# Tridiagonalisation of a 1024 x 1024 matrix in one kernel: other steps for the last two tiles, another order of waits

## What is computed

```python
deg = sum(A, 0) + sum(A, 1) - diagonal(A)
L_norm = dinv[:, None] * (diag(deg) - A) * dinv[None, :]
_, U = eigh(L_norm)
h = relu(einsum('mn,bnd->bmd', U.T, x) @ W1 + b1)
out = einsum('nm,bmd->bnd', U, h @ W2 + b2)
```

## Time and profile before

| | |
|---|---|
| median of 3 runs | 9817.23 us (9799.33 to 9818.49) |
| profiled execution | 9792.26 us, of which the span is 9790.5 us |
| VectorE busy | 7098.8 us (73% of the span) |
| TensorE busy | 5600.1 us (57%) |
| ScalarE, GpSimd busy | 1776.4 us (18%), 1185.3 us (12%) |
| tridiagonalisation | about 900 to 6010 us from the span's start |
| its stages of T = 3, 2, 1 | 4441 to 4977, 4986 to 5505, 5512 to 6005 us |
| granted clock, whole span | 0.746 of 2.4 GHz |

### The profile page before, as it was taken

One profiled execution on the slowest core, in us unless ns is written; L12 is line 12 of the kernel. 1 busy time (PEld: TensorE's weight loads), 2 busy tenths in 40 slices (PEclk: granted clock), 3 DMA queues, 4 the chain that ended last, 5 costly groups with the idle time before them and its releaser, 6 DMA issues. The chain is left out here.

```text
span 9790.5 us, 326141 instructions
## 1 busy us (share of the span) xinstructions
PE 5600.1 (57%) x136408; PEld 3949.5 (40%) x136408; DVE 7098.8 (73%) x33446; ACT 1776.4 (18%) x4691; POOL 1185.3 (12%) x5177
## 2 busy tenths in 40 slices
PE   5675888777878777778777764121111110047866
PEld 2354555555566666566656653010000000033355
DVE  3555666767777777777777778989898989954154
ACT  1432111111111111111111111121111110011055
POOL 0000111111222222222222221000000000000000
PEclk8898999999999999786655555555555555579988
DMA  1000000000000000000000000000000000000000
GB/s 35 1 0 18 4 4 4 4 4 4 4 4 4 4 4 4 4 4 4 4 4 4 3 3 2 0 0 0 0 0 0 0 0 0 0 0 1 17 0 17
DMA packets 24594, 41.92 MB, mean 4 GB/s; under 512 B 2464, under 2 KB 20128, under 8 KB 23200
## 3 DMA queue, kind: packets, MB, share of 16 engines
q1 hardware_dynamic: 23200, 21.70, 0.7%
HBM read 17.50 MB, written 4.19 MB: 2 GB/s over the span
## 5 line engine op out<-in xcount | busy, mean ns | idle before, releaser
L289 PE MATMUL tri_y<-L 128*32 128x256 f32 (+7 forms) x36792 | 1941.3, 343 | 18.7 <-issue 17.7
L289 PEld LDWEIGHTS tri_y<-L 128*32 128x32 f32 x36792 | 1187.9, 122 | 241.9 <-issue 66.3
L1342 PE MATMUL ev_agree<-ev_prod,ev_fold 128*128 128x448 bf16 x520 | 241.3, 567 | 1683.5 <-DVE ev_prod L1465 1666.9
L1342 PEld LDWEIGHTS ev_agree<-ev_prod,ev_fold 128*128 128x128 bf16 x520 | 34.8, 111 | 1887.8 <-DVE ev_prod L1465 1867.4
L314 PE MATMUL tri_ring<-ident 128*128 128x128 bf16 x7414 | 750.3, 268 | 2.1 <-issue 1.9
L1458 DVE SCALAR_TENSOR_TENSOR ev_seq<-ev_seq,ev_ne2G,ev_u 128x112 f32<-128x112 f32 x2048 | 686.1, 335 | 73.3
L1454 DVE SCALAR_TENSOR_TENSOR ev_u<-ev_x,ev_dG,ev_seq 128x112 f32<-128x112 f32 x2048 | 683.9, 334 | 64.0
L272 PE MATMUL tri_k<-tri_kp,tri_half 128*32 128x1 f32 x8176 | 264.8, 189 | 759.7 <-DVE tri_x L476 755.8
L364 ACT ACTIVATE tri_mu<-tri_ring,tri_tiny 128x1 f32<-128x1 f32 x1022 | 267.4, 262 | 2172.6 <-PE tri_ring L272 2172.6
L314 PEld LDWEIGHTS tri_ring<-ident 128*128 128x128 bf16 x7414 | 582.1, 121 | 171.0 <-issue 155.6
L366 ACT ACTIVATE tri_sM<-tri_half_M,tri_s 128x8 f32<-128x8 f32 (+7 forms) x1022 | 304.2, 298 | 1823.4 <-DVE tri_s L468 1823.4
(11 more groups left out here) (615 smaller groups left out, 12957.9 us busy)
## 6 DMA issues: line engine op xcount, KB each, us to landing
adj<-in_adj_dram SPq DMA_DIRECT2D x12, 1024.0 KB, 8.1
x<-in_x_dram SPq DMA_DIRECT2D x8, 512.0 KB, 7.2
out_dram<-x SPq DMA_DIRECT2D x8, 512.0 KB, 6.6
gcn_w<-in_L_gnn_W_dram SPq DMA_DIRECT2D x2, 128.0 KB, 2.1
spec_w<-in_L_gnn_W_dram SPq DMA_DIRECT2D x2, 64.0 KB, 1.9
dot_wt<-in_L_gnn_W_dram SPq DMA_DIRECT2D x1, 64.0 KB, 1.8
dot_rows<-in_L_gnn_b_lin_dram SPq DMA_DIRECT2D x1, 64.0 KB, 2.7
dot_rows<-in_L_gnn_b_dram SPq DMA_DIRECT2D x1, 64.0 KB, 3.7
```

Source lines behind the costliest of these rows:

```text
L289: last = nc.tensor.matmul(y[32 * g:32 * g + 32, 0:T * 32], A[:, b + t, XC:XC + 1].broadcast_to([P, 32]), cols, start=(t == 0), stop=(t == ...
L1342: last = nc.tensor.matmul(agree, fold16[:, :], prod[:, z, h * (GRP // 2):(h + 1) * (GRP // 2), :].rearrange("p s w -> p (s w)"), start=Fal ...
```

## The change

For T of 1 and 2 (`few`) the step is written anew. The norm follows x directly, ahead of w. TensorE makes the sum twice, into two banks (`sigma` for ScalarE, `sigma_v` for VectorE), and then the products, ahead of rows and coefs; there is no filler. The flag is made from the second sum while the root is under way. `sgn2` and `aa` take the place of S2. `rows` and `coefs` stay, BnS goes to GpSimd, whose fB, nB and Bc go away for one product Cf = flag times Cw; fB is now on VectorE, followed by z, q1 = z - Bn and q. Kappa comes from TensorE as a sum of products of gx and t itself, over T matmul groups, and c from gx and zh, which ScalarE makes from t; the half and the flag in them are in `s4[:, s, 1:2]` and `vmc`. One instruction more per panel (kS) scales the kappas. L476 and L479 have no counterpart.

For T = 3 the norm follows x directly too, and one product stands ahead of the sum, as for T of 4 and more already. For all T of 3 and more: the flag is written behind S2; kappa's wait is written ahead of vm's, c's ahead of v's, and on ScalarE inv's ahead of xm's. The numbers of fillers for T = 3 to 6 are unchanged.

The core of the diff:

```diff
+FILL = {6: 8, 5: 10, 4: 10, 3: 10}
...
+        few = lambda T: T <= 2
+        norm_first = lambda T: T <= 3
+        idle = lambda T: FILL.get(T, 0)
...
+                        if few(T):
+                            pool.wait_ge(fl_ready, r + 1)
+                            nc.gpsimd.tensor_scalar(Cf[:, b:NT], Cw[:, b:NT, s], fl[:, s:s + 1], None, ALU.mult).then_inc(Cf_ready, 1)
+                            if s:
+                                pool.wait_ge(sum_ready, r + 1 if s0 else r)
+                                nc.gpsimd.tensor_tensor(col, Cw[:, b:NT, s], rowsum[:, b:NT], ALU.add).then_inc(Bn_ready, 1)
+                        else:
+                            pool.wait_ge(Bn_ready, r + 1)
+                            nc.gpsimd.tensor_scalar(fB[:, b:NT], col, fl[:, s:s + 1], None, ALU.mult).then_inc(pool_step, 1)
+                            pool.wait_ge(pool_step, 3 * r + 1)
+                            nc.gpsimd.tensor_tensor(nB[:, b:NT], fB[:, b:NT], col, ALU.subtract).then_inc(pool_step, 1)
...
-                        early = 0 if T < 4 else 1
-                        for t in range(early):
-                            product(t)
+                        first = T if T <= 2 else 1
+                        if not few(T):
+                            for t in range(first):
+                                product(t)
                         pe.wait_ge(norm_part, r + 1)
                         four(sigma, ones[:, 0:32], part[:, :]).then_inc(norm_ready, 1)
+                        if few(T):
+                            four(sigma_v, ones[:, 0:32], part[:, :]).then_inc(norm_again, 1)
+                            for t in range(first):
+                                product(t)
...
-                        for t in range(early, T):
+                        for t in range(first, T):
                             product(t)
-                        if T <= 6:
-                            for _ in range(8 if T == 6 else 10):
-                                nc.tensor.matmul(ring[3][:, 0:P], S["ident16"][:, :], S["ident16"][:, :], start=True, stop=True)
-                        pe.wait_ge(kappa_part, r + 1)
-                        four(kappa(s), half[:, 0:32], kp[:, :]).then_inc(kappa_ready, 1)
-                        four(c_sum, half[:, 0:32], kp[:, :], stop=False)
+                        for _ in range(idle(T)):
+                            nc.tensor.matmul(ring[3][:, 0:P], S["ident16"][:, :], S["ident16"][:, :], start=True, stop=True)
+                        if few(T):
+                            pe.wait_ge(t_ready, r + 1)
+                            pe.wait_ge(gx_ready, r + 1)
+                            tm = t1 if s else tr[:, 0:NT * 32].rearrange("p (t m) -> p t m", m=32)[:, :, 0]
+                            t0 = b if s else 0
+                            for t in range(T):
+                                last = four(kappa(s), gx[:, b + t:b + t + 1].broadcast_to([P, 32]), tm[:, t0 + t:t0 + t + 1], start=(t == 0), stop=(t == T - 1))
+                            last.then_inc(kappa_ready, 1)
+                            pe.wait_ge(zh_ready, r + 1)
+                            for t in range(T):
+                                four(c_sum, gx[:, b + t:b + t + 1].broadcast_to([P, 32]), zh[:, b + t:b + t + 1], start=(t == 0), stop=False)
+                        else:
+                            pe.wait_ge(kappa_part, r + 1)
+                            four(kappa(s), half[:, 0:32], kp[:, :]).then_inc(kappa_ready, 1)
+                            four(c_sum, half[:, 0:32], kp[:, :], stop=False)
...
-                        act.wait_ge(s4_ready, r + 1)
-                        nc.scalar.activation(sM[:, b:NT], half_M[:, s, 0:T], ACT.Copy, scale=s4[:, s:s + 1]).then_inc(sM_ready, 1)
+                        if not few(T):
+                            act.wait_ge(s4_ready, r + 1)
+                            nc.scalar.activation(sM[:, b:NT], half_M[:, s, 0:T], ACT.Copy, scale=s4[:, s, 0:1]).then_inc(sM_ready, 1)
+                        act.wait_ge(inv_ready, r + 1)
                         act.wait_ge(xm_ready, r + 1)
-                        act.wait_ge(inv_ready, r + 1)
                         nc.scalar.activation(vm[:, b:NT], xm[:, b:NT], ACT.Copy, scale=inv[:, 1:2]).then_inc(vm_ready, 1)
+                        if few(T):
+                            act.wait_ge(s4_ready, r + 1)
+                            act.wait_ge(vm_ready, r + 1)
+                            nc.scalar.activation(vmc[:, b:NT], vm[:, b:NT], ACT.Copy, scale=s4[:, s, 1:2]).then_inc(vmc_ready, 1)
+                            tm = t1[:, b:NT] if s else tr[:, 0:T * 32].rearrange("p (t m) -> p t m", m=32)[:, :, 0]
+                            act.wait_ge(t_ready, r + 1)
+                            nc.scalar.activation(zh[:, b:NT], tm, ACT.Copy, scale=s4[:, s, 1:2]).then_inc(zh_ready, 1)
...
+                    def norm(r):
+                        if r:
+                            dve.wait_ge(x_ready, r)
+                        X = xcol(b)
+                        V_.tensor_tensor_reduce(out=x2[:, act_t], in0=X, in1=X, scale=1.0, scalar=0.0, op0=ALU.mult, op1=ALU.add,
+                                                accum_out=part[:, 0:1]).then_inc(norm_part, 1)
+                    if norm_first(T):
+                        norm(0)
...
+                        if few(T):
+                            pre = r + 1 if s0 else r
+                            dve.wait_ge(pivot_ready, r + 1)
+                            k_sg = mark(V_.tensor_scalar(sg[:, :], pivot(s)[:, 1:2], 0.0, -0.5, ALU.is_ge, ALU.add))
+                            dve.wait_ge(norm_again, r + 1)
+                            V_.tensor_scalar(f1, pivot(s)[:, 1:2], pivot(s)[:, 1:2], sigma_v, ALU.mult, ALU.is_lt).then_inc(fl_ready, 1)
+                            dve.wait_ge(root_ready, r + 1)
+                            mark(V_.reciprocal(rt[:, :], mu[:, :]))
+                            after(k_sg)
+                            mark(V_.tensor_scalar(sgn2[:, :], sigma_v, sg[:, :], None, ALU.mult))
+                            kk = mark(V_.scalar_tensor_tensor(out=aa[:, :], in0=mu[:, :].broadcast_to([P, 2]), scalar=sg[:, :], in1=pivot(s), op0=ALU.mult, op1=ALU.add))
+                            if s:
+                                dve.wait_ge(rows_ready, pre)
+                                k_b = mark(V_.tensor_tensor(c3(prodb), v_w(b)[:, :, :, 0:s], spread(rows(s)), ALU.mult))
+                            after(kk)
+                            kk = mark(V_.scalar_tensor_tensor(out=pair[:, s, :], in0=rt[:, :].broadcast_to([P, 2]), scalar=sgn2[:, :], in1=aa[:, :], op0=ALU.mult, op1=ALU.add))
+                            if s:
+                                dve.wait_ge(coefs_ready, pre)
+                                k_c = mark(V_.tensor_tensor(c3(prodc), v_w(b)[:, :, :, 0:s], spread(coefs(s)), ALU.mult))
+                                after(k_b)
+                                V_.tensor_reduce(rowsum[:, act_t], c3(prodb), mybir.AxisListType.XY, ALU.add).then_inc(sum_ready, 1)
+                            after(kk)
+                            V_.reciprocal(inv[:, :], pair[:, s, :]).then_inc(inv_ready, 1)
+                            if s:
+                                after(k_c)
+                                k_c = mark(V_.tensor_reduce(corr[:, act_t], c3(prodc), mybir.AxisListType.XY, ALU.add))
                             dve.wait_ge(mv_ready, r + 1)
+                            ins = V_.transpose(tr[:, 0:T * 32], y[:, 0:T * 32])
+                            if s:
+                                k_t = mark(ins)
+                            else:
+                                ins.then_inc(t_ready, 1)
+                            dve.wait_ge(inv_ready, r + 1)
+                            V_.scalar_tensor_tensor(out=gx[:, act_t], in0=X, scalar=inv[:, 0:1], in1=H_, op0=ALU.mult, op1=ALU.add).then_inc(gx_ready, 1)
+                            dve.wait_ge(fl_ready, r + 1)
+                            V_.scalar_tensor_tensor(out=s4[:, s, :], in0=one_half[:, :], scalar=inv[:, 0:1], in1=f1.broadcast_to([P, 2]), op0=ALU.mult, op1=ALU.mult).then_inc(s4_ready, 1)
+                            if s:
+                                after(k_t)
+                                V_.tensor_tensor(tm, trc, corr[:, act_t], ALU.add).then_inc(t_ready, 1)
+                                dve.wait_ge(Cf_ready, r + 1)
+                                dve.wait_ge(sum_ready, pre)
+                                k_f = mark(V_.scalar_tensor_tensor(out=fB[:, act_t], in0=rowsum[:, act_t], scalar=f1, in1=Cf[:, act_t], op0=ALU.mult, op1=ALU.add))
+                                after(k_f)
+                                col, colf = BnS[:, s, 0:T], fB[:, act_t]
+                            else:
+                                dve.wait_ge(Cf_ready, r + 1)
+                                col, colf = Cw[:, act_t, 0], Cf[:, act_t]
```

(39 more changed lines are left out.)

134 lines of the change are left out of this document (61 added, 73 removed).

## The result

| | before | after |
|---|---|---|
| median of the timed runs | 9808.36 us (9799.33 to 9818.49) | 9707.43 us (9700.07 to 9721.77) |
| span of the profiled execution | 9790.5 us | 9702.5 us |
| first x of T=8 to first x of T=3 | 3524 us | 3506 us |
| stage of T=3, of T=2, of T=1 | 545, 526, 491 us | 544, 502, 446 us |
| all that follows | 3786 us | 3788 us |

The ratio is 0.9899, with a 95% interval of 0.9881 to 0.9916: 101 us less, where 94 were forecast (9713). A stage is counted here from its first x to the first x of the next one.

A forecast was written before the change was run, and what follows sets the result against it. The prediction took each step as a latency-bound chain across engines. Its terms, 36 (T=2) + 55 (T=1) - 1 (kS) + 9 (waits) - 4 (T=3) = 95 us, from 9807 gave 9713 us; range 9660 to 9768.

The forecast's parts named there:

- Front: From x to L440 at T=2 and T=1: norm no longer stands behind w, gaining 0.17 us a step.
- middle: From L440 to t: instructions and waits go out, gaining 0.19 us at T=2 (s=17) and 0.31 at T=1.
- tail: From t to the next x: a chain of dependent VectorE instructions, losing 0.04 us a step.
- the stall before prodb: At T=2 VectorE waits for rows behind two products: 0.07 us at s=17, growing by 0.2 to 0.25 at large s.
- the small steps' 0.45: At small s of T=2, stall and wide sums vanish and more old dependencies show: gain 0.45 us a step.
- The waits: T above 3: c's wait first lets norm start 0.07 us earlier; bounds 0 and 18 us, middle of 9 taken.
- The split: T=3: gain 0.06 us at the high clock, loss 0.14 less 0.05 at the low; net 4 us lost.
- The thin rebuild: Rival: at T=2 and T=1 the stall for rows and coefs fills the middle's gain; 9770 us, chance 0.08.
- The serial tail: Rival: VectorE's five handoffs from fB to the next norm cost 0.13 us each, not 0.04; 9844 us, slower chance 0.04.
- The order of waits does nothing: Rival: exchanging the waits gains nothing, leaving 82 us in all; 9725 us, chance 0.1.
- The rule: VectorE's next operation waits for an empty pipe; would add 92 us of gain, ending near 9621; given no chance.
- Fillers and flag: Dropping fillers at T=2 and T=1 costs TensorE nothing; writing the flag behind S2 brings 0 us.

The follow-up runs named there:

- e4: Changed kernel with the products put behind rows and coefs at T=2 and T=1; 9706.08 us.
- e6: Changed kernel with ten fillers a step put back at T=2 and T=1; 9724.83 us.
- e9: As e8, but c at T=3 is made from one tile instead of three, so results are wrong; single run 9677.71 us.
- e7: Changed kernel with products behind rows and coefs at T=3 to 1 and norm ahead of w up to T=5; 9686.11 us, ratio 0.9875.
- e1: Changed kernel with everything at T of 3 and more put back, only the T=2 and T=1 steps new; 9724.93 us, ratio 0.9914.
- e11: Kernel before with only the flag moved behind S2 in every step; single run 9812.25 us.
- e2: Kernel before with only the three pairs of waits exchanged, at every T; 9777.45 us, ratio 0.9968.
- e3: Changed kernel with the norm put back behind w at T=2 and T=1; 9731.03 us.
- e8: e7 with the new step at T=3 too, no fillers there, and norm behind w again at T=4 and 5; 9752.8 us, ratio 0.9943.
- e10: As e9, with kappa at T=3 made from one tile as well, so results are wrong; single run 9667.34 us.
- e5: Changed kernel with T=3's first product put back behind rows and coefs, its norm still ahead of w; 9703.25 us, ratio 0.9885.
- e12: e7 with fillers at T=4 only; 9742.71 us, ratio 0.9937.

## Why the prediction was right, and where not

The forecast was 9713 and the range 9660 to 9768; the kernel takes 9707. The parts of the sum, against the stages:

| | forecast | measured |
|---|---|---|
| T=2 | 36 | 24 |
| T=1, with kS | 54 | 45 |
| T=3 | -4 | 1 |
| T above 3 | 9 | 18, by no term of the sum |
| all that follows | 0 | -2 |

The sum of these, 86, stands beside 88 between the two spans. The total is nearer than its parts: two were too high, and the third came out high for reasons that were not in the sum. At T up to 3, where the terms did their work, 86 were forecast and 70 came; that the whole is so near is luck.

**Front, middle, tail.** At s=17 the laid-out step was right to 0.04 at T=2 and 0.02 at T=1. Each of the three sections came within 0.03, the stall before prodb among them. That it grows with s is shown by e4: at s of 12 to 20 moving rows forward brings 0.05, at s of 25 and more 0.21. The forecast of 0.06 to 0.1 for the gain at large s holds, 4.027 to 3.955.

**T=2, 24 for 36.** The failed term is the small steps' 0.45. Undisturbed (again the shortest of the four panels) they gain 0.38 over s=1 to 8, 3.787 to 3.412; the flag holds L492 there too. All undisturbed steps together gain 0.24 for the 0.28 of the sum. The four stalled steps are 6 us more. Nothing in the trace of before told of them: at T=2 it handed TensorE 46 instructions per us (180 in 3.89 us), after 57, which is less than the 58 at T=4, where its matmuls never waited for "issue". That a step's instructions must also be delivered was not a term of the sum; what makes them late at these steps stays open (e6, e9).

**T=1, 45 for 54.** 0.40 a step for 0.43, 49 us; another 4 go at the start of panels, where VectorE gets its first instruction 1.4 us later. (The prediction's own terms, 0.17 + 0.31 - 0.04, make 0.44, not 0.43; that is 1 us.)

**The waits.** At T above 3 the 9 us can't be found. Undisturbed steps differ from before by -0.004, +0.036, -0.016, -0.032 and +0.045 us at T = 8 to 4, in all 0.03 the wrong way, and kernels with the same source differ by as much (4.125 to 4.201 at T=4). The failed step is that c's exchange helps at T of 5 and 4, where the sum might wait for the norm; the prediction took the middle between never and always. The norm does come 0.07 earlier, as forecast, but the sum doesn't. The step s=17 at T=5 shows it, of before and of after:

```profile
3462.44 0.23 DVE L487 SCALAR_TENSOR_TENSOR L<-tri_vm,tri_k,tri_q 128x5 f32<-128x5 f32 x1
...
3462.81 0.46 PE L289 MATMUL tri_y<-L 128*32 128x160 f32 x8
3462.82 0.17 DVE L430 CUSTOM_DVE_ANT_0 tri_x<-L 128x5 f32<-128x5 f32 x1
...
3463.08 0.22 PE L272 MATMUL tri_ring<-tri_part,ones 128*32 128x1 f32 x8
```

```profile
3449.83 0.23 DVE L611 SCALAR_TENSOR_TENSOR L<-tri_vm,tri_k,tri_q 128x5 f32<-128x5 f32 x1
...
3450.14 0.16 DVE L471 CUSTOM_DVE_ANT_0 tri_x<-L 128x5 f32<-128x5 f32 x1
3450.20 0.46 PE L307 MATMUL tri_y<-L 128*32 128x160 f32 x8
...
3450.47 0.22 PE L290 MATMUL tri_ring<-tri_part,ones 128*32 128x1 f32 x8
```

The norm starts 0.38 behind x in before and 0.31 in after; the sum starts at 0.64 in both, behind the early product, which starts at 0.37 in both. In e7 the norm is at 0.27 and the sum at 0.65. Over all steps of T=5 the median start of the sum is 0.65 in all three kernels, and at T=4 the norm goes from 0.37 to 0.31 and 0.27 while the sum stays at 0.60 to 0.59. So the sum goes by what stands ahead of it in TensorE's queue, the early product last, and the lower bound of that term, 0, was the right one.

What the exchanges do bring above T=3 comes by kappa, for which the prediction had no term there. Where kappa ends well behind q, x comes 0.05 to 0.06 earlier: the step s=1 at T=4, at a clock of 0.50, takes 4.49 us in before, e1 and e11 and 4.43 in e2, after and e7. Before has 43 steps at T=4 with a mean clock below 0.72, and only some of them gain so, which makes 2 us at the most (an estimate, 43 x 0.05).

The 18 us lie in long steps. Before has 46 steps at T above 3 that are over 0.5 us above their like in another panel, 47 us in all, after 26 with 24 us. Some 6 us of the difference are TensorE's waits on "issue" within the steps (15 and 8 us). The other long steps that I opened are ones in which the clock drops for a moment, as here at T=8 (a disturbed step, then its neighbour):

```profile
1146.00:1153.80 7.80, 6.58 (x184) 4.46 (x180) 3.31 (x24) 0.76 (x3) 1.14 (x5) 0.78 0.01 2
1153.80:1160.00 6.20, 4.98 (x184) 3.56 (x184) 3.37 (x24) 0.75 (x3) 1.14 (x5) 1.00 0.01 3
```

A step at a mean clock of 0.78 takes 7.8 us, one at 1.00 6.2. The number of long steps changes from kernel to kernel where the source of these stages does not: after, e3 to e6 and e8 to e10, alike there, have 26 to 41 of them and take 3504 to 3531 us from T=8 to T=3. That is not all scatter, though. The three programs written as before is, with the old steps at T=2 and 1 (before, e2, e11), take 3524 to 3541; e1, which has the new steps there but the waits and the flag of before at T above 3, takes 3517; and e2 has the new order of waits and takes 3531. So the order of waits explains 2 us of the 18 at most. What else the rest of the program changes in these stages, no run shows.

At T up to 3 the prediction gave kappa's exchange 0.02 and c's nothing, because there the norm goes ahead of w. e2, in which the norm follows w at every T, shows why both were right: 0.02 at x, 0.06 at w, and the 0.06 are taken over by the norm's move.

**T=3.** The split was right. Norm and waits gain 0.13 a step (e2, e5); the prediction has 0.59 - 0.48 = 0.11 and 0.02. The product ahead of the sum costs 0.14; by the prediction's terms 0.36 x 0.05 + 0.64 x 0.25 = 0.18. So the stage loses next to nothing, and e5, which takes the product back, gains 15 us. The prediction saw that loss and could have named the better order.

**The rivals.** The thin rebuild falls by e1. The serial tail falls by the timeline: z to q1 is 0.25 and q1 to q 0.20, so that each handoff is 0.03 to 0.04 behind the end of the one before (5406.08 + 0.22 to 5406.33), far from the 0.11 at which the sign would turn. "The order of waits does nothing" is false at T up to 3 (e2), and above 3 it moves the norm but, kappa's few steps at T=4 aside, not the step.

**The rule.** In the new step L492 starts at 5404.25 and lasts 0.15, and L494, which doesn't need it, starts 0.08 before its end; z, q1 and q, which need one another, start 0.03 to 0.04 after. The prediction set such rows against the Trainium skill (VectorE: DVE Perf Modes, The DRAIN you can't avoid) and took from it that the next operation waits for an empty pipe. It read the passage too narrowly: the same section says that an operation that is not held starts earlier, and with that the 0.08 agree. The other point that the prediction took from that section of the Trainium skill, that a semaphore costs nothing extra, is measured there on eight copies; here an operation that waits for its neighbour starts 0.12 later than one that doesn't, and the layout, which priced it so, was right to 0.04. The 92 us that the other reading would have added did not come.

**Fillers and flag.** Both at nothing, and both right (e6, e11).

## What to carry to other kernels

When a step is a chain across engines, lay it out from one x to the next, with what a dependent neighbour costs and what an independent one costs; it was good to 0.04 in 3.6 us. Ask of every term that stands between two bounds which engine's queue the instruction goes into and what stands ahead of it there: a wait that ends earlier is worth nothing behind a product that doesn't. Then count the instructions per microsecond that the new step asks of each engine, and compare with the densest stretch of the kernel. Well above it a step can run out of instructions (e8), and the profile shows it as idle time ended by "issue", on single steps at the same places of each panel. A count below it is no assurance (T=2 of after). And read a gain from its stage, not from the whole, where other stages scatter by more than it is worth.

## What the runs showed of the hardware

- TensorE ran dry where steps asked for 72 matmuls and weight loads per us (e8, 52 us in one stage of 128 steps), little at 61 to 64 (one step in each panel of e9 at T=3; some 6 us within the steps of T=6 in e7), and not at 53 (e10 at T=3). The rate is not all of it: at 56 to 58 it stalled in four steps at T=2 (after, e7), in one in e9 with the step of e7, and never at T=4 (before); at 63 it stalled in three, and for less time (e6 at T=2).
- At the start of a panel at T=2 TensorE sat idle for 5.3 to 6.0 us for want of an instruction in before, after and e7. In e9 it was 2.5 to 2.7 us, ended by ScalarE, and the gap between two panels was 2 us shorter.
- A VectorE instruction that needs nothing of its neighbour started 0.08 us before the neighbour's end, one that needs it 0.03 to 0.04 us after (after, s=17 at T=2).
- Of two waits ahead of a VectorE instruction, writing first the one that ends last was worth 0.06 us at w and 0.02 at x (e2).
- Fillers held the granted clock at T=5 (0.93 with, 0.78 without) and were worth 0.32 us a step there; at T=3 they raised it from 0.50 to 0.72 for next to nothing (3.909 to 3.902 us a step, e12 and e7), and at T=2 and 1 they did not raise it (e6).
